# Another order of clearing, weight loads and stores in the prologue of a graph-network kernel

## The reference

```python
h = mish(concat([x[src], x[dst], edge_attr]) @ W1 + b1)
messages = mish(h @ W2 + b2)
agg = segment_sum(messages, dst)
u = mish(concat([x, agg]) @ W3 + b3)
out = u @ W4 + b4
y = layernorm(x + out) * gamma + beta
```

## Time and profile before

| | us |
|---|---|
| median of 3 runs (1329.16 to 1330.71) | 1330.06 |
| the profiled execution | 1334.39 |
| its span in the profile | 1332.7 |
| end of the prologue (next block's first work on ACT) | 108.68 |

### The profile page before, as it was taken

One profiled execution on the slowest core, in us unless ns is written; L12 is line 12 of the kernel. 1 busy time (PEld: TensorE's weight loads), 2 busy tenths in 40 slices (PEclk: granted clock), 3 DMA queues, 4 the chain that ended last, 5 costly groups with the idle time before them and its releaser, 6 DMA issues. The chain is left out here.

```text
span 1332.7 us, 18963 instructions
## 1 busy us (share of the span) xinstructions
PE 1244.3 (93%) x5844; PEld 998.1 (75%) x5844; DVE 1015.5 (76%) x1799; ACT 851.6 (64%) x772; POOL 697.3 (52%) x484
## 2 busy tenths in 40 slices
PE   7974999999999999999999999968799896999998
PEld 6753777777777777787777777756588785888886
DVE  4324799999999999999999999745776247847444
ACT  3204999999999999999999999727633011312210
POOL 0216788888888888888888888117130000011000
PEclk9996999999999999999999999988999997999999
DMA  7997867777877777777777887668200520000001
GB/s 229 329 353 146 169 135 156 154 155 154 159 159 153 149 142 151 155 152 155 155 153 157 159 156 136 193 241 322 85 16 0 190 69 24 17 1 2 0 20 60
DMA packets 108315, 183.59 MB, mean 138 GB/s; under 512 B 35154, under 2 KB 44672, under 8 KB 108248
## 3 DMA queue, kind: packets, MB, share of 16 engines
q0 software_dynamic: 71056, 106.45, 41.4%
q1 hardware_dynamic: 30104, 64.09, 13.9%
q10 hardware_dynamic: 7088, 12.20, 2.8%
HBM read 141.21 MB, written 41.30 MB: 137 GB/s over the span
## 5 line engine op out<-in xcount | busy, mean ns | idle before, releaser
L222 POOL DMA_INDIRECT w_raw<-q_dram,idx_all x172 | 361.1, 2099 | 87.1 <-issue 53.1
L1057 PE MATMUL ps_x<-wA_hi,hT_hi 128*128 128x512 f32 x668 | 270.7, 405 | 1.3 <-DVE hT_lo L747 1.3
L1057 PE MATMUL ps_x<-wA_hi,hT_lo 128*128 128x512 f32 x668 | 264.4, 396 | 0.0
L1057 PE MATMUL ps_x<-wA_lo,hT_hi 128*128 128x512 f32 x668 | 264.1, 395 | 0.0
L222 POOL DMA_INDIRECT w_raw<-p_dram,idx_all x176 | 182.0, 1034 | 109.6 <-issue 108.5
L1057 PEld LDWEIGHTS ps_x<-wA_hi,hT_hi 128*128 128x128 f32 x668 | 125.6, 188 | 34.1 <-issue 2.0
L1057 PEld LDWEIGHTS ps_x<-wA_hi,hT_lo 128*128 128x128 f32 x668 | 125.5, 188 | 30.1
L1057 PEld LDWEIGHTS ps_x<-wA_lo,hT_hi 128*128 128x128 f32 x668 | 125.5, 188 | 28.3
L756 DVE TENSOR_TENSOR x<-ps_x,b 128x512 f32<-128x512 f32 x167 | 114.0, 683 | 26.8 <-PE ps_x L1057 23.0
L1692 POOL TENSOR_TENSOR tmp_n<-X,gam 128x512 f32<-128x512 f32 x10 | 13.9, 1394 | 224.9 <-DVE t_be L1777 180.3
L1016 PE MATMUL ps_x<-ident,w_raw 128*128 128x128 f32 x672 | 103.7, 278 | 20.2 <-issue 12.5
(11 more groups left out here) (270 smaller groups left out, 2858.1 us busy)
## 6 DMA issues: line engine op xcount, KB each, us to landing
ea_raw<-in_eaT SPq DMA_DIRECT2D x88, 128.0 KB
adj_dram<-adj_sb POOLq DMA_DIRECT2D x42, 210.2 KB
adj_dram<-agg_sb ACTq DMA_DIRECT2D x11, 640.5 KB
U_lo<-adj_dram SPq DMA_DIRECT2D x10, 640.0 KB, 8.7
adjT_dram<-adjT_sb SPq DMA_DIRECT2D x10, 640.0 KB, 7.9
adjT_rest<-adjT_dram SPq DMA_DIRECT2D x7, 640.0 KB, 10.0
w_raw<-in_w SPq DMA_DIRECT2D x4, 1024.0 KB, 8.0
w_raw_g<-in_w SPq DMA_DIRECT2D x4, 1024.0 KB, 7.7
```

What stands on the lines that cost most here:

```text
L222: g.indirect_dma_start(G[:, slot, c * D:(c + 1) * D], None, rows, bass.IndirectOffsetOnAxis(ap=idx_all[:, i:i + 1], axis=0), **op).then_in ...
L1057: last = t.matmul(ps_x2[c % 2][:, :], h[:, b.slot, e], w[:, k, :], start=(k == 0 and i == 0), stop=(k == KD - 1 and i == 2))
```

## The change

In the prologue, x's third tile is loaded ahead of the index rows, and four tiles are then under way at a time instead of two. The clearing is cut in two: counts' memory is cleared from right after W0a's split, two blocks at once and one behind each evacuation of P; sums' memory beside Q. w03 is loaded into the first half of `w_raw` and split beside P's products, where W02's split was; W02, W0c, b02 and b03 are loaded later, and W02 is split beside Q. The turned x is stored behind Q's last store, in two pieces of 1.5 MB instead of twelve. POOL's first gathers wait in addition for w03's split, since they write where it lies.

Behind the edge work, two of the four tiles of z0 are loaded at the end of `edge_phase`; the two others, gam, bet and W_l's bias, and also w1r, are loaded by SP at step 5 of the first layer's ten (where the last counts are loaded, r = R - 1); of the vectors only b4 stays ahead of step 0. POOL waits for b4 alone, and issues w1l's load after its fifth addition.

```diff
-CLEAR_FROM = 3
+X_AHEAD = 4
...
+                load_x(2)
...
-                def store_p(r):
+                load_x(3)
+                for r in range(X_AHEAD, R):
+                    sp.wait_ge(x_in[r - X_AHEAD], 16)
+                    load_x(r)
+                sp.wait_ge(w_lo_ready, KD)
+                sp.dma_start(w_raw[:, 0:KD, :], by_slices(w03[0:D, :])).then_inc(w3_in, 16)
+                for r in range(R):
                     sp.wait_ge(p_evac, r + 1)
                     store(p_dram, r, r, st_out[r % OUTS])
-
-                for r in range(2, R):
-                    sp.wait_ge(x_in[r - 2], 16)
-                    load_x(r)
-                    if r == 6:
-                        store_p(0)
-                for r in range(1, R):
-                    store_p(r)
-                    if r == 1:
+                    if r == 3:
+                        sp.dma_start(b1[:, :], bcast(b01)).then_inc(b_in, 16)
+                    if r == 5:
                         sp.dma_start(w2_raw[:, :, :], by_slices(w02)).then_inc(w2_in, 16)
                         for half in range(2):
                             sp.dma_start(wc_raw[half * ED:(half + 1) * ED, :], w0c).then_inc(w2_in, 16)
-                    if r == 3:
-                        sp.dma_start(b1[:, :], bcast(b01)).then_inc(b_in, 16)
+                    if r == 7:
                         sp.dma_start(b2[:, :], bcast(b02)).then_inc(b2_in, 16)
                         sp.dma_start(b3[:, :], bcast(b03)).then_inc(b3_in, 16)
-                sp.wait_ge(w2_low, KD)
-                sp.dma_start(w2_raw[:, :, :], by_slices(w03[0:D, :])).then_inc(w3_in, 16)
                 for r in range(R):
                     m = R + r
                     sp.wait_ge(q_evac, r + 1)
                     store(q_dram, r, m, st_out[m % OUTS])
                     if r < 2:
                         load_edge_attr(sp, ea_raw, eaT, r, r, ea_in[r])
-                    if r >= R - ZE:
-                        i = r - R + ZE
-                        for to, part in zip(xT_dram, (xT_hi, xT_lo)):
-                            sp.dma_start(to[:, cols(i)], part[:, i, :].bitcast(F32)).then_inc(xT_out, 16)
+                for to, part in zip(xT_dram, (xT_hi, xT_lo)):
+                    sp.dma_start(to[:, :], part[:, 0:ZE, :].rearrange("p r d -> p (r d)").bitcast(F32)).then_inc(xT_out, 16)
                 for r in range(ZE, R):
                     sp.wait_ge(z_evac, r - ZE + 1)
                     store(z0_dram, r - ZE, 2 * R + r - ZE, z0_out)
                 for u in range(OUTS):
                     sp.wait_ge(st_out[u], 16 * (2 * R // OUTS))
-                sp.wait_ge(xT_out, 32 * ZE)
+                sp.wait_ge(xT_out, 32)
                 sp.wait_ge(b2_in, 16)
...
+                wait(w3_low, KD)
...
-                        dve_.wait_ge(w2_split, k + 1)
-                        v.tensor_tensor(w2_lo[:, k, :], w2_raw[:, k, :], w2_hi[:, k, :].bitcast(F32), ALU.subtract).then_inc(w2_low, 1)
-                dve_.wait_ge(w2_split, KD + 1)
-                v.tensor_tensor(wc_lo[:, :], wc_raw[:, :], wc_hi[:, :].bitcast(F32), ALU.subtract)
+                        dve_.wait_ge(w3_split, k + 1)
+                        v.tensor_tensor(w3_lo[:, k, :], w_raw[:, k, :], w3_hi[:, k, :].bitcast(F32), ALU.subtract).then_inc(w3_low, 1)
                 dve_.wait_ge(b_in, 16)
                 for r in range(R):
                     m = R + r
                     slot_free(dve_, m)
                     dve_.wait_ge(m_out, m + 1)
                     v.tensor_tensor(o_sb[:, m % OUTS, :], ps_o[m % 2][:, :], b1[:, :], ALU.add).then_inc(q_evac, 1)
-                    if R - KD <= r:
-                        k = r - R + KD
-                        dve_.wait_ge(w3_split, k + 1)
-                        v.tensor_tensor(w3_lo[:, k, :], w2_raw[:, k, :], w3_hi[:, k, :].bitcast(F32), ALU.subtract).then_inc(w3_low, 1)
+                    if 1 <= r <= KD:
+                        k = r - 1
+                        dve_.wait_ge(w2_split, k + 1)
+                        v.tensor_tensor(w2_lo[:, k, :], w2_raw[:, k, :], w2_hi[:, k, :].bitcast(F32), ALU.subtract).then_inc(w2_low, 1)
+                    if r == 1 + KD:
+                        dve_.wait_ge(w2_split, KD + 1)
+                        v.tensor_tensor(wc_lo[:, :], wc_raw[:, :], wc_hi[:, :].bitcast(F32), ALU.subtract)
...
-                def clear(r):
+                def clear_counts(r):
                     act.dma_start(adj_dram[r * P:(r + 1) * P, :].rearrange("p (q n) -> p q n", q=NQ),
                                   zeros[:, 0:NC].rearrange("p (q n) -> p q n", q=1).to_broadcast([P, NQ, NC])).then_inc(zero_out, 16)
-                    act.dma_start(agg_dram[r * P:(r + 1) * P, :], zeros).then_inc(zero_out, 16)
+
+                def clear_sums(r):
+                    act.dma_start(agg_dram[r * P:(r + 1) * P, :], zeros).then_inc(zero_agg, 16)
...
+                act.wait_ge(z_ready, 1)
+                clear_counts(0)
+                clear_counts(1)
                 for r in range(R):
                     if 1 <= r and r + 1 < R:
                         x_high(r + 1)
                     if r >= R - KD:
                         high(2 * KD + r - R)
                     if 1 + KD <= r < 1 + 2 * KD:
-                        k = r - 1 - KD
-                        if k == 0:
-                            act.wait_ge(w2_in, 48)
-                        a.copy(w2_hi[:, k, :], w2_raw[:, k, :]).then_inc(w2_split, 1)
-                    if r == 1 + 2 * KD:
-                        a.copy(wc_hi[:, :], wc_raw[:, :]).then_inc(w2_split, 1)
+                        if r == 1 + KD:
+                            act.wait_ge(w3_in, 16)
+                        a.copy(w3_hi[:, r - 1 - KD, :], w_raw[:, r - 1 - KD, :]).then_inc(w3_split, 1)
                     slot_free(act, r)
                     act.wait_ge(m_out, r + 1)
                     a.copy(o_sb[:, r % OUTS, :], ps_o[r % 2][:, :]).then_inc(p_evac, 1)
                     if r == 1:
                         act.dma_start(w_raw[:, KD:, :], by_slices(w0b)).then_inc(w_in[KD], 16)
-                    if r == 2:
-                        act.wait_ge(z_ready, 1)
-                    if r >= CLEAR_FROM:
-                        clear(r - CLEAR_FROM)
-                for r in range(R - CLEAR_FROM, DROWS // P):
-                    act.wait_ge(m_out, r + CLEAR_FROM + 1)
+                    if r + 2 < DROWS // P:
+                        clear_counts(r + 2)
+                act.wait_ge(w2_in, 48)
+                for r in range(DROWS // P):
+                    if r < KD:
+                        a.copy(w2_hi[:, r, :], w2_raw[:, r, :]).then_inc(w2_split, 1)
+                    if r == KD:
+                        a.copy(wc_hi[:, :], wc_raw[:, :]).then_inc(w2_split, 1)
+                    act.wait_ge(m_out, R + r)
                     act.sem_inc(turn, 1)
-                    clear(r)
-                act.wait_ge(w3_in, 16)
-                act.sem_inc(turn, 1)
-                for k in range(KD):
-                    a.copy(w3_hi[:, k, :], w2_raw[:, k, :]).then_inc(w3_split, 1)
+                    clear_sums(r)
...
+                sp.wait_ge(lo_ready, n * (NB * 2))
+                sp.wait_ge(z0_out, 16 * (R - ZE))
+                for r in range(ZE, 2 * KD):
+                    sp.dma_start(Z[r][:, :], z0_dram[(r - ZE) * P:(r - ZE + 1) * P, :]).then_inc(z_in[r - ZE], 16)
                 for r in range(ZE):
                     sp.wait_ge(xT_in[r], n * 32)
...
-                            wait(zero_out, 32 * (DROWS // P))
+                            wait(zero_out, 16 * (DROWS // P))
                             wait(shifted, p + 1)
...
+                        if b.k == 0:
+                            wait(zero_agg, 16 * (DROWS // P))
...
-                            dve_.wait_ge(zero_out, 32 * (DROWS // P))
+                            dve_.wait_ge(zero_out, 16 * (DROWS // P))
+                            dve_.wait_ge(zero_agg, 16 * (DROWS // P))
...
                     if s == 0:
-                        sp.wait_ge(z0_out, 16 * (R - ZE))
-                        for r in range(ZE, R):
-                            sp.dma_start(Z[r][:, :], z0_dram[(r - ZE) * P:(r - ZE + 1) * P, :]).then_inc(z_in[r - ZE], 16)
-                        for t, b in ((b4, b04), (gam, g0), (bet, be0)):
-                            sp.dma_start(t[:, :], bcast(b)).then_inc(vec_in, 16)
+                        sp.dma_start(b4[:, :], bcast(b04)).then_inc(b4_in, 16)
...
+                    if r == R - 1:
+                        for i in range(2 * KD, R):
+                            sp.dma_start(Z[i][:, :], z0_dram[(i - ZE) * P:(i - ZE + 1) * P, :]).then_inc(z_in[i - ZE], 16)
+                        for t, b in ((gam, g0), (bet, be0), (bl, b1l)):
+                            sp.dma_start(t[:, :], bcast(b)).then_inc(vec_in, 16)
+                        sp.wait_ge(w4_lo, KD)
```

(15 more changed lines are left out.)

19 lines of the change are left out of this document (10 added, 9 removed).

## The result

The change makes the kernel 0.43% faster: 1323.85 us against 1330.11 us in the median of 13 runs each, ratio 0.9957 with a 95% interval of 0.9946 to 0.9969, some 5.7 us by the ratio and 6.3 by the medians. The forecast was a gain of 14 us, 1316 us. The time lies inside the range given (1304 to 1325), near its upper end. That pair looks better than the medians because before's profiled execution lay 4.3 us above its median and the one after 0.3 us above.

What follows compares the result with a forecast made beforehand. PE is busy 93% of the span; the prologue is limited by transfers that begin late. Prologue -10 and first layer -4 make -14 from 1334.39, so 1320.4, less 4.3 for the median: 1316.1 us; range 1304 to 1325.

Steps and rivals of the forecast that it cites:

- Transfers beside P: Prologue, up to P's end: +4.8 us of added transfers against 4.4 us of idle DMA time filled; taken as 0.
- PE's second wait for x: Prologue, x's third tile: PE's 1.9 us lost there go; x's loads worth 0 to -3.5 us at this point.
- Beside Q: Prologue: 14 us fewer transfers leave Q bound by PE at 2.71 us per product, last evacuation 75.4 not 85.5; -10 us.
- Q's last store: Prologue: no turned x ahead in its queue, so evacuation's end to POOL's start falls from 9.6 to 6 us; -3.6.
- Behind Q: Prologue's tail: two stores of turned x (9.2 us) run beside the gathers and z0's stores; 0 to +9, taken +4.
- a block's end held by turned x's stores: Prologue's end: listed among the signs in the changed profile that would show the forecast wrong; no size given.
- The second way: Prologue check: 10.2 us of unused DMA time, less 3.3 still open, plus z0's stores (3.1), is also 10.
- First layer: First layer: up to -6 at step 2, 4.5 given back at step 5, -2.3 at a later wait; -4, bounds -9 and +2.
- w1l follows five of POOL's additions: First layer: w1l issued after five additions (1.33 us each) instead of ten, into full engines; part of the 4.5 us given back.
- should go: -2.3: First layer: the wait of 2.26 us at 929.30, behind w1l and w1r, should go; -2.3 us.
- more than that: Rival: P runs at PE's pace and the first layer keeps its -7.4; -16 - 9 = -25, 1305 us; chance 0.15.
- only a part pays: Rival: step 5's transfers cost step 2's gain, DVE's wait for W02's halves costs 3 us; -7, 1323 us; chance 0.23.

Runs made afterwards that it cites:

- gated layer: New first layer with GpSimd's last five additions of b04 held until VectorE has split W04; against the kernel before, 0.9974 behind the old prologue, 0.9926 to 0.9940 behind the new.
- without the early start: Against the gated kernel with P's first two stores ahead of w03: no two counts clearings at W0a's split, all eleven start at P's first evacuation; 0.9894 of before.
- the layer alone: The changed first layer behind the old prologue, POOL not held back, against the kernel before: ratio 1.0009 (0.9992 to 1.0026).
- the second job: Job that ran the changed kernel again, unaltered, beside each half alone and one with POOL held back; changed kernel 0.9982 of before, median 1326.56 us.

## Why the prediction was right or wrong

The forecast was a gain of 14 us and the measured one is 5.7. Two steps of the working failed: in the first layer the place of POOL's second five additions was put at nothing, and in the prologue P's end was put at 0 and came 2.9 us later. The stretches of all profiled executions with the same code, means in us (old prologue: 4 executions; new prologue: 10; for the layer, old 3, new 4, the gated layer 9, under either prologue and its variants):

| stretch | old | new | moved | forecast |
|---|---|---|---|---|
| to P's last evacuation | 48.3 (47.4 to 49.6) | 51.2 (48.8 to 52.6) | +2.9 | 0 |
| from there to Q's last | 34.9 (33.9 to 37.6) | 27.4 (27.2 to 28.1) | -7.5 | -10 |
| to the first gather with accumulation | 11.2 | 4.1 | -7.1 | -3.6 |
| to the edge phase's table load | 12.8 | 16.9 | +4.1 | +4 |
| prologue | 107.1 (104.7 to 108.7) | 99.5 (97.6 to 101.4) | -7.6 | -10 |
| edge phase | 767.7 | 767.5 | -0.2 | 0 |
| first layer, to u_high(0) | 61.1 (59.9 to 62.1) | 59.8 (57.2 to 64.0) | -1.2 | -4 |
| the same without the hold | | 56.3 (54.8 to 58.5) | -4.8 | -4 |

- *Transfers beside P, 0.* Mis-sized, within its bounds: +2.9. The idle time was filled as forecast ("of the idle 7 us at least 12.2 to 15.5 is filled, 4.4 in all"; share 0.98). The step that failed is to take this as 4.4 us off P's stretch. The early clearing runs beside x's loads: PE's second wait for x, which was to go, is 2.0 to 4.5 us in the ten executions and 1.7 to 2.2 in the old ones, and 0.5 us in the one execution without the early start, whose P ended at 47.90. ACT's wait of 4.5 to 7.5 us for P's first store, behind w03, was not in the sum either.
- *Beside Q, -10.* The mechanism was right: no evacuation waits for a store of Q, and the last ones are 2.72 us apart. Q's stretch came down to the forecast 27 us. The gain is smaller because its start was read from one execution, in which Q took 37.6 us behind P; three others took 33.9 to 34.0. ACT's halves of W02 cost nothing, as forecast.
- *Q's last store, -3.6.* Right direction, too small: in the profiled pair 9.6 became 3.85 us. In the mean this and the term before make -14.6, where -13.6 was forecast; that the two errors nearly cancel is luck.
- *Behind Q, +4.* Right: with turned x's stores beside Q the tail was 3.4 us shorter. The prediction also lists "a block's end held by turned x's stores" among the signs of being wrong, which doesn't fit this term. The profiled pair's prologue came out at -10.4 against -10, but only because its terms missed in both directions.
- *The second way.* That the unused DMA time less what stays open also gave 10 was a coincidence: the run without the early start left DMA time unused (share 0.59) and lost nothing. The Trainium skill's rule that all queues share the same 16 engines ("DMA: Bandwidth & Descriptors", "Issuing engines are not separate DMA queues") doesn't say that filling the gap shortens the rest.
- *First layer, -4.* This is the step that failed most: it came out at +1.8 in the profiled pair and about -1 in the mean, and the layer alone gave nothing in the time (1.0009). "w1l follows five of POOL's additions" was costed as a transfer only; that the other five would then run into the split of W04 on DVE was put at nothing without a reason. The runs showed the split held for 4.2 to 6.9 us and PE waiting 1.3 to 4.7 us behind it. With POOL held back, the new layer alone is at 0.9974 (-3.5 us), and the whole kernel at 0.9926 to 0.9940 instead of 0.9954 to 0.9982.
- *The layer's other terms* were not right singly. Step 2's wait shrank by 3.4 us. The wait of 2.26 us at step 7, which "should go: -2.3", became 4.18 us, and 2.0 to 3.5 in the gated kernels. Step 5 took a new wait of 3.57 us. That wait is for the store of step 3, ahead of the transfers that the prediction put at step 5; it is 1.6 and 2.0 us in the two kernels that issue w1l last, so part of it is w1l's. That the gated layer still gains 4.8 us comes for the larger part from PE's clock (46.6 us of work in the mean of nine instead of 49.5), of which the prediction counted up to 1.9 us. So its nearness to -4 is partly luck.
- *The sum.* -14 was worked out against an execution 4.3 us above its median. I took the 4.3 off the time, but not off the gain. Of this excess 1.5 us lay in the prologue and 1.1 in the layer (108.68 and 62.13 against means of 107.1 and 61.1), where the change could remove it. In the rival "more than that", the "-7.4" for the first layer is worked out nowhere; its sum uses the bound of -9.
- What stays open: the stretches in the mean make -9.0, the three ratios of the changed kernel -5.7, -2.4 and -6.1 us. Profiled executions aren't average ones: that of the second job was the fastest of its kernel, 1319.29 us against a median of 1326.56. The rival "only a part pays" (-7, 1323 us) named the right time by luck: of its two causes, W02's halves cost nothing, and of the transfers at step 5 only a longer wait at step 7 was seen, 4.18 instead of 2.26 us.

## What to carry to other kernels

When a DMA issue is moved forward in an engine's queue, ask also where the instructions behind it end up: here five additions off the critical path landed beside a split on it, and cost about what the rest of the layer's change won (+1.2 us by the ratio, -3.5 with POOL held back, in two jobs). A wait that costs nothing (POOL until the split is done) gives it back; with P's first two stores ahead of w03 as well, the kernel runs at 0.989 to 0.990 of the one before, 1317.54 and 1318.03 us in two jobs, the best version here, with or without the early clearing (1316.10 us). That is the 14 us of the forecast, but only with two edits that the predicted kernel doesn't have. When a long wait of PE is split into short ones, count the clock too: here it was worth more than the waits. And read a length that the forecast rests on from several executions, or take its excess off the gain as well.

## What the runs showed of the hardware

- A VectorE operation with both operands in SBUF (W04's split, 0.68 us alone) took up to 1.71 us when it began inside a series of GpSimd's additions, one addition being 1.25 us. Inside the first such series of the changed kernel (879.20 to 885.92) the degree's TENSOR_REDUCE at 881.57 kept its 1.47 us. The Trainium skill, "SBUF — State Buffer", section "Who interferes with whom", says that a DVE instruction with two SBUF inputs contends with a GpSimd instruction that reads SBUF, and that the port pair which the two share is an exclusive lock. These lengths agree with that. The four holds of 4.17 to 6.94 us don't follow from a lock held for one instruction: they lasted up to five additions, and the one of 6.94 us is recorded as begun 0.15 us ahead of the series (886.57 against 886.72). All four met a series that GpSimd began right behind the issue of a transfer.
- PE's granted clock in the first layer's ten steps was 0.84 and 0.85 in the three executions of the old layer, with 49.1 to 49.7 us of PE's work in 259 records, and 0.86 to 0.92 in the nine gated ones, with 45.4 to 49.1 us. Behind a wait of 4.30 us the ten matmuls that turn the counts took 2.37 us, behind one of 2.46 us they took 1.28.
- DMA share at or above 1 went with 314 GB/s in one execution and 344 in another from 20 to 48 us, and 357 and 400 from 48 to 84 us. One of the two begins its clearing later, so the mix of transfers in these windows differs.
- The same code ended P between 48.8 and 55.0 us in twelve executions. That the prologue's transfers fall in another order each time would explain it, but this was not followed up.
